# Two-layer cross-attention on one core: the second half of layer 1's LayerNorm is queued later on ScalarE and on GpSimd

## The reference

```python
q = emb @ Wq + bq                # 224 x 512
k = latent @ Wk + bk             # 750 x 512
v = latent @ Wv + bv
w = softmax(q @ k.T / sqrt(512), axis=tokens)   # over the 224 tokens, for each context row
x = w @ v + emb
return (x - mean(x)) * rsqrt(var(x) + EPS) * gamma + beta
```

## Time and profile before

| What | Value |
|---|---|
| Time, median of 3 runs | 1000.95 us (1000.65 to 1000.99) |
| The profiled execution's own time | 1000.18 us |
| Its span, first to last instruction | 998.4 us |
| TensorE busy | 975.7 us, 98% |
| VectorE busy | 859.5 us, 86% |
| ScalarE busy | 760.2 us, 76% |
| GpSimd busy | 766.1 us, 77% |
| Granted TensorE clock | 0.998 of full speed |
| DMA | 98.37 MB, mean 99 GB/s |

### The profile page before, as it was taken

One profiled execution on the slowest core, in us unless ns is written; L12 is line 12 of the kernel. 1 busy time (PEld: TensorE's weight loads), 2 busy tenths in 40 slices (PEclk: granted clock), 3 DMA queues, 4 the chain that ended last, 5 costly groups with the idle time before them and its releaser, 6 DMA issues.

```text
span 998.4 us, 25754 instructions
## 1 busy us (share of the span) xinstructions
PE 975.7 (98%) x7300; PEld 910.6 (91%) x7300; DVE 859.5 (86%) x2602; ACT 760.2 (76%) x2128; POOL 766.1 (77%) x709
## 2 busy tenths in 40 slices
PE   7999999999999999999999999999999999999997
PEld 6889999999999999999999999999999999999986
DVE  5888988988888988888888888898888898888867
ACT  3667887777887777887777787777788777788764
POOL 0437788887888787878778878787878878888884
PEclk9999999999999999999999999999999999999999
DMA  7754443554344454343455344455444455434101
GB/s 207 178 104 103 98 102 89 106 116 98 82 101 97 95 112 99 82 104 94 93 112 104 83 99 100 86 112 106 85 99 97 86 112 111 94 91 103 37 17 50
DMA packets 358998, 98.37 MB, mean 99 GB/s; under 512 B 308648, under 2 KB 342821, under 8 KB 358949
## 3 DMA queue, kind: packets, MB, share of 16 engines
q1 hardware_dynamic: 356405, 96.98, 43.8%
q10 hardware_dynamic: 2544, 0.80, 0.4%
HBM read 83.06 MB, written 14.68 MB: 98 GB/s over the span
## 4 chain that ended last, share of the span: by engine, by line
PE 90%; DVE 3%; SPq 2%; issue 2%; ACT 1%; POOL 1%; DMA 1%; DVEq 0%; ACTq 0%; POOLq 0%
PE oq_bank L787 9%; PE score_bank L743 9%; PE score_bank L748 8%; PE score_bank L744 8%; PE oq_bank L797 6%; PE pv_bank L834 6%; PE oq_bank L772 6%; PE pv_bank L836 6%; PE pv_bank L843 6%; PE oq_bank L720 5%; PE oq_bank L715 5%; PE oq_bank L716 5%; PE oq_bank L773 5%; PE t_bank L672 2%; PE oq_bank L810 1%
## 5 line engine op out<-in xcount | busy, mean ns | idle before, releaser
L1083 ACT ACTIVATE probs<-probs,neg_max 125x224 f32<-125x224 f32 x378 | 177.8, 473 | 94.2 <-DVE neg_max L1523 94.2
L743 PE MATMUL score_bank<-qT_hi,cT_hi 128*125 128x224 f32 x768 | 196.2, 282 | 5.9 <-issue 4.1
L744 PE MATMUL score_bank<-qT_hi,cT_lo 128*125 128x224 f32 x768 | 188.3, 272 | 0.0
L1927 POOL TENSOR_TENSOR p_lo<-probs,p_hi 125x672 fp32r<-125x672 f32 x60 | 98.3, 1638 | 84.6 <-DVE p_hi L1559 84.6
L1111 ACT ACTIVATE probs<-probs,rsum 125x224 f32<-125x224 f32 x378 | 153.7, 474 | 1.4 <-DVE rsum L1543 1.4
L743 PEld LDWEIGHTS score_bank<-qT_hi,cT_hi 128*125 128x125 f32 x768 | 144.7, 188 | 10.6 <-issue 9.3
L1523 DVE CUSTOM_DVE_ANT_0 probs<-score_bank,d_row 125x224 f32<-125x224 f32 x384 | 139.2, 382 | 10.2 <-PE score_bank L748 6.6
L748 PE MATMUL score_bank<-qT_lo,cT_hi 128*125 128x224 f32 x768 | 147.2, 273 | 0.7 <-DVE qT_lo L1506 0.7
L744 PEld LDWEIGHTS score_bank<-qT_hi,cT_lo 128*125 128x125 f32 x768 | 144.8, 189 | 0.0
L772 PE MATMUL oq_bank<-p_hi,raw_hi 125*128 125x224 f32 x480 | 140.6, 318 | 0.0
L715 PE MATMUL oq_bank<-xT_hi,A_hi 128*128 128x224 f32 x512 | 120.8, 275 | 0.3 <-ACT xT_hi L1055 0.2
(11 more groups left out here) (169 smaller groups left out, 2907.1 us busy)
## 6 DMA issues: line engine op xcount, KB each, us to landing
cb<-in_ctx_dram SPq DMA_DIRECT2D x248, 92.0 KB
raw<-in_ctx_dram SPq DMA_DIRECT2D x31, 500.0 KB
x<-in_x_dram SPq DMA_DIRECT2D x32, 448.0 KB, 4.0
xb<-in_x_dram SPq DMA_DIRECT2D x124, 112.0 KB, 2.7
out_dram<-y_out SPq DMA_DIRECT2D x31, 448.0 KB, 4.2
raw<-in_ctx_dram SPq DMA_DIRECT2D x62, 125.0 KB
cb<-in_ctx_dram SPq DMA_DIRECT2D x124, 3.5 KB
y<-in_L_xattn_Wq_dram SPq DMA_DIRECT2D x2, 512.0 KB, 5.4
```

The lines of the kernel that those rows point to most:

```text
L743: nc.tensor.matmul(o, cT_hi[:, u.slot, l, cols], qT_hi[:, l, :], start=(l == 0), stop=False)
L744: nc.tensor.matmul(o, cT_lo[:, u.slot, l, cols], qT_hi[:, l, :], start=False, stop=False)
L1083: ins = act.activation(probs[0:MP, u.par4, c, :], probs[0:MP, u.par4, c, :], ACT.Exp, bias=neg_max[0:MP, u.par4, c:c + 1], scale=-1.0, acc ...
```

## The change

Two steps of the layer-1 unit `b(-2)`, both of token half 1, get another place in their engine's turn. Nothing is added or removed.

```diff
@@ ScalarE's turn @@
                 standardise(b(-2), 0)
-                standardise(b(-2), 1)
                 ctxT_hi(a(+0), 0)
                 exps(b(-1), 1)
                 q_hi(a(+0), 0)
                 normalise(b(-1), 0)
                 normalise(b(-1), 1)
+                standardise(b(-2), 1)
                 ctxT_hi(a(+0), 1)
@@ GpSimd's turn @@
                 a, b = units(i, j)
-                scale(b(-2), 1)
                 add_beta(b(-2), 0)
                 probs_lo(b(-1))
                 last_probs_lo(b(-1))
                 inverse_deviation(a(-1))
+                scale(b(-2), 1)
                 sum_thirds(b(-1))
```

## The result

The changed kernel takes **1012.4 us**, median of the runs, against 1000.8 for the kernel before on the same chip: a ratio of 1.0118, with a 95% interval of 1.0101 to 1.0136. That is 11.6 us slower. The forecast was 1010.0 us, in a range of 1000 to 1020. The profiled execution took 1012.38 us with a span of 1010.6; the granted clock of TensorE was 0.999 in it.

A forecast was written before the change was run, and what follows sets the result against it. The prediction took TensorE, waiting for late `p_lo`, as the bound, with a second chain through VectorE setting 30.0 us turns. Terms 4.4 + 0 + 4.5 = 8.9 us on 1000.95 gave 1010.0 us, range 1000 to 1020.

The forecast's parts named there:

- First term: ScalarE's `exps` and `normalise` start earlier, so GpSimd's last `p_lo`, which TensorE waits for, ends 0.55 us earlier each turn.
- the short chain alone: Rival: VectorE's `dot`s are not held up, so turns are 0.55 us shorter, 985 us in all; chance 0.12.
- GpSimd 1.3 later: On GpSimd, everything behind the moved gamma pass, sums, raw parts and both `scale(a, h)`, comes 1.3 us later.
- The collision: GpSimd's late `scale` passes and VectorE's `dot`s exclude each other; the second `dot` ends 0.94 us later.
- Length of the turn: The chain through VectorE grows by 0.4 us, making every turn 30.0 us, whatever its kind.
- How the delay reaches the next `score_max`: Through the reciprocal, `normalise(a, 1)`, `q_hi(b, 1)` and `q_lo(b, 1)`, the turn's last `score_max` comes 0.4 us later.
- Where TensorE waits: At L787 of `o_product(a, 0)`, TensorE waits for ScalarE's `normalise(a, 1)`, 0.3 to 0.8 us a turn.
- Size: Over 29 turns, 4.4 + 0 + 4.5 = 8.9 us longer in sum.
- The harder collision: Rival: GpSimd's second pass goes straight on, both `dot`s come behind it; 10 us more, 1019 us; chance 0.13.
- The softer collision: Rival: VectorE gets both `dot`s in before GpSimd's second pass, or the shift is overrated; 995 to 1003 us; chance 0.15.
- No effect: Rival: nothing waits for the moved half and the kernel is bound elsewhere, so time is unchanged; chance 0.02.

The follow-up runs named there:

- kernel 5: Changed kernel, plus GpSimd waiting for both `dot`s of b before the second `scale` of a, and `inverse_deviation(b)` ahead of the sums of a; 986.3 us against 1001.3.
- kernel 9: Kernel before, plus GpSimd's wait for b's `dot`s before the second `scale` of a and `inverse_deviation(b)` ahead of the sums of a; 1001.1 us against 1000.8.
- Experiment 3: Changed kernel with the moved gamma pass cut to 8 of its 512 columns; 991.9 us, ratio 0.9908.
- experiment 6: Kernel before with only GpSimd's `inverse_deviation(b)` put ahead of the sums of a; 1001.1 us, ratio 0.9996.
- experiment 1: Kernel before with GpSimd's half of the change alone, the gamma pass of token half 1 behind `rstd`; 1011.7 us against 1001.3.
- experiment 2: Kernel before with ScalarE's half of the change alone, `standardise` of token half 1 behind `normalise(b(-2+1), 1)`, that is `normalise(b(-1), 1)`; 1152.6 us, ratio 1.1552.
- experiment 7: Changed kernel with the moved gamma pass one place earlier, ahead of `inverse_deviation(a)`; 994.8 us, ratio 0.9930.
- experiment 4: Changed kernel, plus GpSimd waiting for both `dot`s of b before the second `scale` of a; 1010.7 us, ratio 1.0103.

## Why the prediction was right, and where it was not

**First term, 0.55 a turn at the last `p_lo`: right.** It was to end 6.0 behind the last `score_max`; it ends 5.89 behind. The gain is real: kernels 5 and 9, which differ by the change alone, are 15 us apart. That this is near the 29 x 0.55 = 16 worked out for the short chain alone is partly luck: in kernel 9 `p_lo` is 0.4 us later than in the kernel before, by its held-up cast, and in kernel 5 it ends 6.3 to 6.5 behind the `score_max`, not 5.9.

**GpSimd 1.3 later: right.** The idle time ahead of `rstd` was to be 0.89 and is 1.08, or 0.96 in the turns with the jump; the `x` passes were to start 7.5 behind `rstd` and start 7.51 behind. Experiment 3 shows that this shift causes the loss: 20 us come back when the pass takes 0.2.

**The collision: right in kind and size.** Second `dot` 1.65 forecast, 1.66 measured; it ends at 542.93, 0.56 behind the passes' end at 542.37, where 0.55 had been taken from the opening. The two passes take 0.45 more than before, for 0.46. By the Trainium skill's rule taken literally the turn would have been longer again; the row decided, and the measurement sides with it. Full durations one behind the other give 534.32 + 0.75 + 1.28 + 0.75 = 537.10, 0.50 behind the sum's 536.60 and 14.5 us in 29 turns, where the prediction says 0.55 and 16. The Trainium skill (SBUF — State Buffer, section Who interferes with whom) also has `cast` and `tensor_scalar` in its list of VectorE operations that can contend. The traces agree, with 0.95 to 1.14 for the cast in experiments 6 and 9 (0.50 when free) and 1.00 for `ve` here (0.16 when free). The prediction had not looked for these.

**Length of the turn: right.** 30.0 was forecast for every turn. The last `score_max`s of b are 30.00 to 30.08 apart, but for the very last, 30.25, where most were 29.6, 30.0 and 29.4.

**How the delay reaches the next `score_max`: right in size, wrong in its last part.** The prediction has it go through `q_lo(b, 1)`, behind which VectorE hardly pauses. That `q_lo` starts 545.45 - 524.51 = 20.94 behind the `score_max`, before 538.85 - 518.22 = 20.63: 0.31 later. The next `score_max` is 0.44 later. Between the two lies `ve`, which took 0.87 before and now takes 1.00, since it falls under GpSimd's sum L1962. Before:

```profile
542.39 0.87 DVE L1643 TENSOR_SCALAR ve<-mv 112x2 f32<-112x2 f32 x1
```

```profile
541.61 1.62 POOL L1962 TENSOR_TENSOR psum<-probs 125x672 f32<-125x672 f32 x1
```

In every turn but the last, in both kernels, `ve` ends 0.02 to 0.03 behind the sum, and the next last `score_max` starts 4.54 to 4.60 behind it, with VectorE idle for 0.04 in between. The sum stands on GpSimd behind the last `p_lo` of a, which waits for `normalise(a, 1)`, and that is late as forecast. So the path is `normalise(a, 1)`, `p_lo`, `add_beta`, `raw_lo_part`, sum, `ve`, `score_max`. The same 4.54 to 4.60 is found in experiments 1, 2, 3 and 7, with turns of 29.3 to 36.5 us; and it is why freeing a `dot` alone gave nothing in experiment 4.

**Where TensorE waits: wrong.** The prediction put it "at L787 of `o_product(a, 0)` for `normalise(a, 1)`", "0.3 to 0.8 us a turn". It waits at that product's first matmul, L772, for VectorE's `q_lo(b, 0)`: `o_product(a, 0)` writes the PSUM bank that `q_lo(b, 0)` reads. That `q_lo` stands on VectorE behind the two `dot`s, the cast, the reciprocal and one `add_pv`, so it is late by the same 0.4: it ends 544.44 - 524.51 = 19.93 behind the `score_max`. TensorE is there after 544.15, the end of its four L720, and stands still for 0.44. The wait is 0.38 to 0.77 in the turns without the jump, as forecast since both waits have one cause, but only 0.07 to 0.19 in those with it. The forecast wait never happens: L787 has no idle time ahead of it in the whole run.

**Size: 2.4 us short.** Between the first and the last of the 30 last `score_max`s that bound these 29 turns lie 871.66 us, before 860.36: the turns add 11.3, not 8.9. Of the difference, 1.3 come from 27 middle turns of 30.05 instead of 30.0. The other 1.1 come from the first and the last turn, which the sum took at 29.36 like the other unrolled ones: they had been 28.67 and 29.22, and are 30.06 and 30.25. Another 0.9 us lies ahead of the turns: the first `dot` of the earlier trace rows starts at 49.80 instead of 48.88, where the code is the same in both kernels. It is not the change: in experiments 6 and 9, which take as long as the kernel before, that `dot` starts at 49.79 and 50.02. So it comes with the execution that was profiled.

**The rivals.** The short chain alone (985) is ruled out for the changed kernel; kernel 5, with two more steps, came to 986.3. The harder collision (1019) did not come: no `dot` on `z` of the changed kernel takes over 1.68, and a `dot` that comes during one pass always gets in ahead of the next. The softer collision is ruled out by the same rows: in none of the 29 turns does VectorE get both `dot`s in ahead of GpSimd's second pass. No effect is ruled out.

## What to carry to other kernels

Moving work off one engine's chain shifts everything behind its new place on the in-order engine; follow that queue to the next instructions that can't run beside one of another engine (here a gamma pass and a `dot`), and not only to the next semaphore. A loss found that way need not condemn the change: the same move cost 11.6 us and gave 15 us, and the difference was one wait and one moved step, both in GpSimd's queue. And a collision can be removed without any gain where the engine that it held up next waits for the other one anyway, so take the trace again before the next step.

## What was not expected of the hardware

A gap of 3.41 us on TensorE, once a turn (experiment 2), was followed by about three and a half microseconds at 1.2 GHz, 1.7 us of clock short, and in 7 of 29 turns by twice that. A gap of 0.44 us, in the changed kernel, left it at 2.4 GHz (0.999 over the run).

What a GpSimd pass holds up on VectorE is more than `dot`s: one `cast` took 1.14 instead of 0.50, and a `tensor_scalar` on 112x2 elements 1.02 instead of 0.16. Other instructions of VectorE under such passes kept their times, as the score reductions at 0.38 that read PSUM. The trace has no wait row for it; only the length of the instruction shows it.
